# Value-product groups of an attention step, joined in two pairs

## What is computed

```
h   = layernorm(x) * (1 + ca) + sa
q, k, v = h @ Wq.T, h @ Wk.T * scale, h @ Wv.T          # 16 heads of 8
attn = softmax(where(causal, q . k, -inf))
x   = x + ga * (layernorm(attn @ v) * gamma + beta) @ Wo.T
h   = layernorm(x) * (1 + cb) + sb
x   = x + gb * (sum over the 2 chosen experts of weight * down(silu(gate(h)) * up(h)))
```

## Time and profile before

| | us |
|---|---|
| median of 3 runs | 651.88 |
| lowest and highest | 650.87 and 654.47 |
| the profiled execution | 650.15 |
| its span, first to last instruction | 648.4 |
| PE busy in the span | 570.3 |
| DVE busy | 465.3 |
| ACT busy | 402.5 |
| POOL busy | 244.3 |

### The profile page before, as it was taken

How to read it: one execution, slowest core, us unless ns; L and a number is a source line. 1 busy time by engine, 2 the same in 40 slices (tenths; PEclk the granted TensorE clock), 3 DMA queues, 4 the chain that set the end, 5 groups by cost and what they waited for, 6 DMA issues and landing times.

```text
span 648.4 us, 16200 instructions
## 1 busy us (share of the span) xinstructions
PE 570.3 (88%) x5145; PEld 413.1 (64%) x5146; DVE 465.3 (72%) x1592; ACT 402.5 (62%) x716; POOL 244.3 (38%) x328
## 2 busy tenths in 40 slices
PE   3679999899999999999999986999878999999940
PEld 1245555555555556455555543999877999999940
DVE  3788777688778778887887773687675666666636
ACT  3505777586777767876876776675644556565512
POOL 6201301032452533533614335355545333333326
PEclk9999999899999999999999999999999999999985
DMA  6544568535253253353252101112241211111138
GB/s 173 187 108 147 153 194 261 161 107 188 60 172 105 77 178 85 98 187 92 89 188 60 52 14 48 30 35 55 56 117 52 59 49 49 49 46 45 42 111 297
DMA packets 66117, 69.37 MB, mean 107 GB/s; under 512 B 9620, under 2 KB 57108, under 8 KB 66052
## 3 DMA queue, kind: packets, MB, share of 16 engines
q1 hardware_dynamic: 61156, 57.46, 30.4%
q0 software_dynamic: 4320, 8.99, 4.4%
q10 hardware_dynamic: 576, 2.10, 0.8%
HBM read 36.92 MB, written 31.03 MB: 105 GB/s over the span
## 4 chain that ended last, share of the span: by engine, by line
PE 58%; DMA 9%; DVE 9%; ACT 9%; issue 7%; POOL 3%; SPq 2%; another core or an unknown queue 1%; ACTq 0%; POOLq 0%; DVEq 0%
PE psN L759 16%; PE psO L541 8%; PE psO L770 8%; PE psN L507 5%; PE psT L522 5%; ACT probs L887 4%; DMA k_parts_dram<-kparts 3%; DMA kst_all<-k_parts_dram 3%; PE psT L524 3%; PE psN L509 3%; DVE negm L1134 2%; PE psM L567 1%; PE psM L549 1%; DMA qst_all<-mrow 1%; PE psM L571 1%
## 5 line engine op out<-in xcount | busy, mean ns | idle before, releaser
L1134 DVE TENSOR_REDUCE negm<-psN 128x1 f32<-128x512 f32 (+3 forms) x352 | 214.9, 635 | 59.2 <-PE psN L509 57.1
L887 ACT ACTIVATE probs<-psT 128x512 f32<-128x512 f32 x320 | 183.9, 596 | 67.2 <-PE psT L524 66.6
L759 PE MATMUL psN<-probs 128*128 128x128 f32 x1136 | 141.0, 277 | 2.9 <-ACT probs L1009 2.3
L759 PEld LDWEIGHTS psN<-probs 128*128 128x128 f32 x1136 | 134.2, 194 | 3.8 <-issue 3.6
L1759 POOL DMA_INDIRECT expert_out<-kst_all,dest x71 | 69.2, 975 | 112.2 <-DVE kst_all L1530 107.5
L522 PE MATMUL psT<-qst_all,kst_all 74*128 74x256 bf16 (+2 forms) x384 | 100.2, 279 | 11.0 <-ACT probs L887 8.3
L507 PE MATMUL psN<-kst_all,qst_all 74*128 74x256 bf16 (+2 forms) x384 | 103.1, 288 | 6.3 <-DMA kst_all<-k_parts_dram 5.2
L541 PE MATMUL psO<-probs,vaug 128*32 128x512 f32 (+3 forms) x1024 | 95.8, 447 | 0.3
L509 PE MATMUL psN<-kst_all,qst_all 117*128 117x128 bf16 x512 | 93.6, 228 | 0.0
L1009 ACT ACTIVATE probs<-gu_w 128x1024 f32 x71 | 74.9, 1056 | 23.8 <-PE psN L759 19.0
L1506 DVE TENSOR_TENSOR probs<-probs,psN 128x512 f32<-128x512 f32 x71 | 48.7, 685 | 53.8 <-PE psN L759 27.6
(11 more groups left out here) (235 smaller groups left out, 721.2 us busy)
## 6 DMA issues: line engine op xcount, KB each, us to landing
q_parts_dram<-qparts SPq DMA_DIRECT2D x24, 384.0 KB, 3.5
k_parts_dram<-kparts SPq DMA_DIRECT2D x24, 384.0 KB, 3.6
qst_all<-q_parts_dram SPq DMA_DIRECT2D x32, 288.0 KB
kst_all<-k_parts_dram SPq DMA_DIRECT2D x32, 288.0 KB
kst_all<-dispatched SPq DMA_DIRECT2D x71, 66.0 KB
xall<-in_x SPq DMA_DIRECT2D x8, 256.0 KB, 4.1
gu_w<-in_gateT SPq DMA_DIRECT2D x4, 512.0 KB, 5.0
gu_w<-in_upT SPq DMA_DIRECT2D x4, 512.0 KB, 5.7
```

Of the source, the lines that this page charges most:

```text
L759: mm = pe.matmul(bank[par][:, c * P:(c + 1) * P], ew[par][:, half, c * P:(c + 1) * P], xgT[par], start=True, stop=True)
L887: nc.scalar.activation(probs[:, g % 2, 512 * u:512 * (u + 1)], psT[:, u % TBANKS, :], ACT.Exp, scale=SOFTMAX_SCALE).then_inc(exp_done, 1)
L1134: nc.vector.tensor_reduce(dst, src, axis=AX.X, op=ALU.max, negate=True).then_inc(nat_done, 1)
```

## The change

Value groups of a step used to lie one by one: group 0 at k = 9 of the step itself, groups 1, 2 and 3 at k = 1, 3 and 5 of the next step. Now groups 0 and 1 lie together at k = 10 of their own step (behind the last `nat`, ahead of `project_q` or `experts` where the step has one), and groups 2 and 3 together at k = 2 of the next step (k = 3 in g = 2), right behind `turn_values`. On ACT `keep_values` moves from k = 6 to k = 4, ahead of `keep_max` where both are at k = 4, and `place_v` from k = 7 to k = 5. In the last step group 1 lies ahead of the last `turn_values(L, 2)` and not behind it.

```diff
@@ step, PE
-                    if k in (1, 3, 5) and there(b, g, -1):
-                        values(*step_at(b, g, -1), (k + 1) // 2)
-                    if k == 9:
+                    if k == (3 if g == 2 else 2) and there(b, g, -1):
+                        values(*step_at(b, g, -1), 2)
+                        values(*step_at(b, g, -1), 3)
+                    if k == 10:
                         values(b, g, 0)
+                        values(b, g, 1)
@@ after the steps, PE
-            for c in range(1, TB):
+            for c in range(2, TB):
                 values(L, 3, c)
@@ step, ACT
-                    if k == 6 and there(b, g, -1):
+                    if k == 4 and there(b, g, -1):
                         keep_values(*step_at(b, g, -1))
-                    if g == 0 and k == 7 and has_earlier(b):
+                    if g == 0 and k == 5 and has_earlier(b):
                         place_v(b)
```

## The result

The changed kernel took 676.5 us (median of 6 runs, 673.96 to 679.22), the kernel before 651.67 in the same sitting (650.87 to 654.55): a ratio of 1.0371, 95% interval 1.0338 to 1.0404. The forecast was 647.8 with 639 to 656 around it. The sign is that of the rival in which bursts starve ACT; its 655.5 us, 3.8 above the kernel before, is 15% of the 24.8.

What follows compares the result with a forecast made beforehand. PE, ACT and DVE were taken to hand on the lead, with the keys' transfer as fixed piece. 650.15 less 3.0 (six batches) less 1.1 (8 other steps) is 646.05; plus 1.73 to the median, 647.8 us; range 639.0 to 656.0.

Steps and rivals of the forecast that it cites:

- the rival in which bursts starve ACT: Joined groups hold scores back beyond psT's two banks, ACT idles at step borders; 655.5 us, chance 0.25.
- ACT's full stretch: In g = 3 ACT has no idle row from 305.63 to beyond 311.92; taken to come 0.8 us earlier.
- What the change saves on PE: Joins save 0.235 us for pair 0 and 1, 0.18 for 2 and 3; 12.9 us over 31 steps.
- Where the saving lies: Following four engines from g = 2 to project_k: a batch gets 0.5 us shorter, not 1.66; six batches 3.0 us.
- g = 3: ACT full; with unit 0 in time its stretch comes 0.8 us earlier, otherwise 0.3 us later; the first was taken.
- g = 2: Without group 1 at k = 1, unit 2's exponential and lnT come 0.9 us earlier, unit 7's exponential 0.6.
- Other edits: keep_values at k = 4: The early takeout waits for nothing; would cost 0.48 us only if ACT were full, as in g = 3, already so.
- PE is the bound: Rival: PE bounds nearly everywhere, so all 12.9 us of its saving arrives; 639.0 us, chance 0.22.
- Nothing: Rival: keys' transfer and ACT's stretch take turns setting the batch, savings become PE waits; 651.9 us, chance 0.15.

Runs made afterwards that it cites:

- set 4: Against the kernel before (632.82 us), all with scatters apart: first pair alone 0.999, changed kernel with late takeout 1.012, changed kernel 1.033; also second pair at k = 5, 0.999.
- sets 3 and 5: Unchanged changed kernel run again beside the kernel before: 675.33 us (1.035) and 677.16 us (1.042).
- set 1: Changed kernel with scatter gates at units 4, 6, 8, 10: 664.82 us (1.025); second pair alone 1.026, first pair alone 1.010, kernel before with those gates 0.998.
- late set: Group of runs where PE's completions come late near scatters in a row; the kernel before took 649.6, 652.9 and 650.7 us in the three such sets.

## Why the prediction was wrong

Three steps failed: that the early takeout costs nothing, that ACT's full stretch comes earlier with the second pair, and that PE's saving reaches the end at all. In set 4, where nothing is late, the first is worth 16.2 us (1.3 a batch, the rest with the clock), the second 6.7, the third all of the 7.3 us that the first pair should save.

**What the change saves on PE** held in each number that the traces show: 1.65 for 1.64, 0.79 and 0.58 as said. By the slots 12.9 us of PE's work are saved; the page's busy time, with modelled ends and more time at 1.2 GHz, does not show it (574.3 for 570.3). None of it reached the end. The nearest clean test, first pair alone with scatters apart, saves 0.235 us in 31 steps, 7.3 us by the slots, and gave 0.999 and 1.000 of the time before, 2.7 us less at the lowest end of the two intervals.

**Where the saving lies** failed, in g = 2 and g = 3.
- *g = 3.* I weighed two cases, unit 0 in time or unit 0 as late as unit 1, and took the first "because the late stretch moves away from the scores". It moved onto them: unit 0 was 1.12 us late before, and 1.63 after. The order was argued from starts (scatters 0.6 us earlier, scores 0.3 later), without knowing how far behind the third scatter the lateness reaches. In this trace it ends with the exponential at 272.38, 1.3 us behind the last scatter's end (270.12 + 0.96). Spacing the scatters is worth 1.5 us a batch (46.9 to 45.4, from sets 3 and 5 to set 1). But it is a small term of the loss, because the kernel before pays for late completions as well: its g = 3 went from 11.1 to 10.1 by the spacing. Between the two kinds of set the kernel before differs by 20 us (632.8 and 652.9), and so does the changed one (655.0 with scatters apart, 675.3).
- *ACT's full stretch.* I saw that ACT is full in g = 3 and counted on its coming earlier. The second pair opened a hole in it instead, 0.53 us, since two banks cover the wait of about one exponential and one x_norm, not 1.33 us. The gap of 1.2 to 1.4 us was in my rival, at a price of 0.6 us a batch. In g = 3 it measured 0.64; the other steps, which the rival left out, add 0.5.
- *g = 2.* lnT was to come 0.9 us earlier in its step. It starts 2.92 us behind the first scores (261.51 less 258.59) where it was 3.12 (295.40 in the earlier trace rows less 292.28): 0.2. Units 0 and 1 start 0.84 us behind their matmuls here at the median (0.45 before), and not for a late completion: ACT is still on four `onn` and edbid of its own queue, up to 259.69 us, which the bullet left out.

**Other edits: keep_values at k = 4** is the step that cost most, as set 4 shows. In a late set its removal brought only 0.7% of the time (675.33 to 670.66 us), for g = 3 then ran at 1.2 GHz in part. That "it waits for nothing" was right, and not the question; it is what waits for it. I looked at g = 3, where the instruction "was in the same chain already", but being in the chain behind unit 6 and ahead of unit 5 are different things: what PE does in between decides. In g = 2 and g = 3 PE waits for unit 5's exponential ahead of unit 7's scores, in g = 0 for mrow ahead of `project_k`. The text even gave the price, 0.48 us where ACT is full; it measured 0.49 in g = 2, 0.48 in `project_k`, 0.43 in g = 3, 1.3 us in a batch. The error was to ask whether ACT is full, and not whether PE stands with two full banks when oT comes, just behind the idle time that the second pair makes.

**The rivals.** "Starved" had the sign and the place: PE's `L522` waits at unit 2, and the exponentials of units 0 and 1 start together (272.38, x2), as its signs were named. It lacked the takeout (2.5% in set 4, 16.2 of 638.87), and the clock, of which the prediction took 1.00 for granted. The Trainium skill's sentence on it ("TensorEngine Tiling (Array Packing)", PSUM Bottleneck) held in kind, but not as a question of load: ACT is busy for 60% of the span after and 62% before. What counts is when it is idle. "PE is the bound" is excluded: 7.3 us saved for one pair, and some twice that for two with the second at k = 5, moved nothing. "Nothing" is what the pairs come to, if they are put where ACT does not notice, though its two reasons (the keys and ACT's stretch taking turns) were not what showed: at k = 5 it was the wait for psM.

**Open** are the cause of the two kinds of set, what within the chip holds the completions back, and why PE's saving is taken up so fully with the first pair alone; the wait for psM explains 2.8 us of PE's waiting in 220 us, the rest was not followed. Open too is why the clock falls more often in some of these kernels.

**No better kernel.** The best ratios are 0.998 (before, scatters apart), 0.999 (first pair) and 0.9986 (both, second at k = 5), and each interval holds 1.

## What to carry to other kernels

Work joined on one engine makes a longer silence for the one behind it: set the length of the burst against buffers times the consumer's time for one (here two times 0.49 us), and look at where the consumer has no slack afterwards. A consumer's extra instruction moved earlier cost its full length here (0.49 us) because its producer stood with full buffers just then; look for the producer's work that needs no buffer and put it beside that. An engine whose time you shorten pays only if the engines that take turns with it have nothing else to wait for: try one part alone before adding up all parts.

## What the runs showed of the hardware

- Two or three indirect DMAs of GpSimd in a row, 0.96 us each with 0.30 to 0.36 between, go with completions of PE that reach ACT 1.1 to 2.1 us after the matmul, up to 1.3 us behind the last DMA's end, in three sets of five; with 1.6 us between them it was 0.25 us. In the other two sets it was 0.26 to 0.33 us beside DMAs as close, so something else has a part in it, which no run shows.
- The same kernel took 632.5 or 652.9 us by the set, more than most edits here.
- With PE waiting 1.79 to 1.86 us in an otherwise busy step the clock fell to 1.2 GHz in five steps of five, with 1.67 to 1.77 us in three of ten, with 1.36 to 1.41 us in three of fifteen; one step then took 1.59 us longer.
- Joining two value groups saves 0.14 us of slot: 128 and 256 columns took 0.79 us joined in every trace that has them, for 0.36 and 0.57 apart, and 512 and 384 took 1.64 to 1.65, for 1.00 and 0.79. The 0.09 us of entry is an estimate from the gap at 282.11.
